# First half of the features turned and measured at the end of layer 1's attention block, with the count of fine targets between two tiles of the running count

## The chip, the cores and the metric

The kernel is one program on one core of a Trainium2 chip. The metric is device microseconds of one execution; several runs are taken and their median is compared. TensorE is called PE, VectorE DVE, ScalarE ACT, GpSimd POOL, and SyncE, which issues most transfers, SP.

## The reference

Four graph layers are applied one after the other to x (2048 nodes, 256 features, fp32), each followed by a residual and a layer norm. The adjacency matrix is 2048x2048. What matters here is the second layer (layer 1 in the code) and the start of the third:

```python
# layer 1: graph attention, 8 heads of 32 features
e = leaky_relu(s_dst[:, None, :] + s_src[None, :, :], 0.2), masked by adj
attn = softmax(e, axis=1)
h_prime = einsum('ijh,jhd->ihd', attn, Wh).reshape(n, 256)
mean, var = mean(h_prime, axis=0), var(h_prime, axis=0)      # over the 2048 nodes
h_prime = relu(gamma * (h_prime - mean) * rsqrt(var + EPS) + beta)
x = layernorm(x + h_prime)
# layer 2: only the first 64 neighbours of each node count
keep = (adj > 0) & (cumsum(adj > 0, axis=1) <= 64)
...
# layer 3: mean over all neighbours, two products, relu
```

## The kernel before, in words

Names: P = 128 partitions, T = 16 tiles of 128 nodes, KT = 2 halves of 128 features, NC = 4 column pieces of CW = 512. `edge` holds the turned adjacency matrix in fp8. `hp` (tile `cur`) is h_prime with nodes on partitions. PSUM is one tile, `banks`, of eight banks of 512 fp32 columns, shared from layer 1 on.

**Blocks.** The program is a row of blocks: `attention` (layer 0), `general_attention` for layer 0, `layer1`, `general_attention` for layer 1, and `tail` (the batch norm of layer 1, its layer norm, and layers 2 and 3). Inside a block each engine has its own instruction queue, written by hand, and waits only on semaphores. Between two blocks all five engines meet at a barrier. `general_attention` is a fallback which runs only if the number `doubt` is 1; with the given inputs each engine loads `doubt`, skips the block's body and goes on.

**End of `layer1`.** For each of 8 heads, PE makes 2 halves of 128x132 and 128x66 products (L997, L1004); the first half of the nodes sums in banks 0 to 3, the second in banks 4 to 7. DVE joins the pieces of each half (`join_pieces`, L1121), which is what frees the half's banks (semaphore `evac`, "pieces_joined"). `divide` (L1136 to L1139) divides heads 0 to 6 by their sums and writes them to `hp` while the last head is still being made; `finish_last` joins and finishes head 7 (L1149 to L1154), and makes `fine`, a column that tells whether every sum of a row is large enough. `count_fine` (L98) sums `fine` over the partitions with a product by ones, DVE turns the result into `doubt` (L1157).

**The running count.** For layer 2, `Cumulation` finds for every pair whether it is among the first 64. For tile t, PE adds `tri` x edge (`up_to_source`, L1715) to four banks, ACT compares two banks at a time through a steep Sigmoid (`compare`, L1729, two ACTIVATEs a tile), and PE then adds `above` x edge (`cumulate`, L1721) and the next tile's L1715 to the same bank. So tiles go in order around a loop ACT, PE, ACT. AHEAD = 2 tiles are compared at the end of `layer1`, the other 14 in the tail. Before the change the four banks are banks 0 to 3.

**Start of `tail`.** SP loads gamma (L1349) and beta (L1351). PE turns the first 128 features of `hp` for all nodes, 16 transposes of 128x128 fp32 into banks 4 to 7 (`turn_features`, L1364); DVE takes the statistics of each bank (`feature_stats`, L1515) and joins them (L1517); POOL takes the root of the variance (L1650, L1652); DVE makes scale and shift (`feature_factors`, L1521 to L1527); ACT applies them with Relu into `hpT` (`apply`, L1464, two ACTIVATEs a half). Then the same for the second 128 features. After that a loop over node tiles s: `back` turns `hpT` back (L1373), DVE adds the residual (L1532) and takes the layer norm, PE turns the result (L1383) and projects it (L1394), while ACT compares tile s + 6 (LEAD = 6).

ACT's queue at the start of the tail is: compare tile 2, apply the first features, compare tiles 3 to 5, apply the second features, then the loop.

## Time and profile before

| | |
|---|---|
| runs | 869.05 us median of 3 (868.21 to 869.98) |
| the profiled execution | 870.34 us |
| its span, first to last instruction | 868.6 us |
| PE busy | 810.2 us (93%) |
| DVE busy | 691.6 us (80%) |
| ACT busy | 568.3 us (65%) |
| POOL busy | 148.5 us (17%) |
| mean granted clock of TensorE | 0.988 |

The span is the time between the first and the last instruction; the execution's own time is 1.74 us longer. Busy shares are averages over all blocks. All times in rows are microseconds from the span's start; a name such as `PE banks L1364` is engine, tile written and line of the kernel before. In brackets behind an instruction stands how long its engine had been idle, and who released it.

### The profile page before, as it was taken

How to read it: one execution, taken by the hardware profiler on the slowest of the kernel's cores; microseconds unless marked ns; L12 is line 12 of the kernel's file. 1: busy time of each engine (PE TensorE's matmuls, PEld its weight loads, DVE VectorE, ACT ScalarE, POOL GpSimd, SP SyncE). 2: the span in 40 equal slices, each digit the busy share in tenths (PEclk: the TensorE clock that was granted, in tenths of full speed). 3: DMA queues.
4: the chain of work that ended last, by engine and by line, in shares of the span. 5: the costliest groups of instructions: out<-in, count | busy, mean ns of one | idle time of the engine just before them, and what ended most of it. 6: DMA issues, size and time to landing. Idle time of an engine off the chain costs nothing. (4 is left out here: it accounts for less than half of the span.)

```text
span 868.6 us, 18889 instructions
## 1 busy us (share of the span) xinstructions
PE 810.2 (93%) x7820; PEld 507.0 (58%) x7820; DVE 691.6 (80%) x1053; ACT 568.3 (65%) x568; POOL 148.5 (17%) x287
## 2 busy tenths in 40 slices
PE   3899999999999999995869999999968999999997
PEld 1334444333444434342559999999943557777786
DVE  6686989899998989897789999999943585555444
ACT  6798989897777767672369999999848630111000
POOL 2511011753110010000420000000001352111122
PEclk9999999999999999998999999999999999999999
DMA  8965344393302020001221111111000000000011
GB/s 291 263 197 169 110 137 144 95 246 85 99 16 58 1 61 1 14 1 37 85 86 52 51 32 48 32 48 48 3 1 1 1 1 1 1 1 1 2 49 49
DMA packets 28615, 56.85 MB, mean 65 GB/s; under 512 B 5808, under 2 KB 10032, under 8 KB 27120
## 3 DMA queue, kind: packets, MB, share of 16 engines
q1 hardware_dynamic: 24400, 46.19, 17.2%
q0 software_dynamic: 4128, 9.44, 4.1%
q8 instruction: 62, 1.02, 0.5%
q14 instruction: 25, 0.20, 0.1%
HBM read 38.70 MB, written 2.23 MB: 47 GB/s over the span
## 5 line engine op out<-in xcount | busy, mean ns | idle before, releaser
L484 ACT ACTIVATE ex<-scores_ps,shift 128x1024 f32<-128x1024 f32 x256 | 262.4, 1129 | 77.7 <-PE scores_ps L344 69.9
L555 DVE TENSOR_TENSOR esum<-esum,ex 128x1024 f32<-128x1024 f32 x192 | 222.9, 1211 | 7.1 <-ACT ex L484 7.1
L340 PE MATMUL scores_ps<-qst,kst 128*128 128x512 f32 x512 | 201.3, 474 | 2.9 <-ACT ex L484 2.2
L997 PE MATMUL banks<-fx,pos 128*128 128x132 f16 x2048 | 160.3, 221 | 7.1 <-DVE pos L1174 6.8
L1267 ACT ACTIVATE steps<-a_all,big_b_head 128x2048 fp8e5<-128x2048 f32 x86 | 163.6, 1988 | 0.0
L344 PE MATMUL scores_ps<-edge,negI 128*128 128x512 fp8e5 x512 | 155.3, 385 | 0.0
L340 PEld LDWEIGHTS scores_ps<-qst,kst 128*128 128x128 f32 x512 | 89.8, 189 | 70.9 <-ACT ex L484 19.8
L997 PEld LDWEIGHTS banks<-fx,pos 128*128 128x128 fp8e5 x2048 | 121.3, 98 | 8.0 <-issue 6.5
L1004 PE MATMUL banks<-fm,edge 128*128 128x66 f16 x2048 | 104.1, 193 | 0.0
L1004 PEld LDWEIGHTS banks<-fm,edge 128*128 128x128 fp8e5 x2048 | 86.6, 98 | 0.0
L1174 DVE TENSOR_TENSOR pos<-steps,edge 128x1024 int32<-128x1024 int32 (+1 forms) x65 | 77.4, 1202 | 2.4 <-PE banks L997 2.2
L344 PEld LDWEIGHTS scores_ps<-edge,negI 128*128 128x128 bf16 x512 | 29.7, 99 | 70.1 <-issue 70.1
L555 DVE TENSOR_TENSOR esum<-ex 128x1024 f32<-128x1024 f32 x32 | 38.9, 1221 | 32.8 <-ACT ex L484 32.5
L1394 PE MATMUL banks<-w,xT_ring 128*128 128x512 f32 x128 | 60.4, 594 | 0.7 <-DVE own L1558 0.6
L359 PE MATMUL mixed_total_ps<-ex,cur 128*32 128x512 f32 x512 | 58.2, 595 | 0.0
L359 PE MATMUL mixed_total_ps<-ex,v 128*32 128x512 f32 x512 | 58.2, 595 | 0.0
L1407 PE MATMUL banks<-y_halves_second,edge 128*128 128x256 f16 x512 | 56.7, 273 | 0.5 <-DVE y_halves_second L1552 0.5
L1407 PEld LDWEIGHTS banks<-y_halves_second,edge 128*128 128x128 fp8e5 x512 | 50.0, 98 | 8.7 <-issue 2.3
L284 POOL DMA_DIRECT2D qst<-high_low x56 | 27.6, 503 | 159.7 <-PE scores_ps L344 138.8
L1407 PE MATMUL banks<-y_halves,kept_rest 128*128 128x256 f16 x448 | 52.0, 273 | 0.5 <-DVE y_halves L1552 0.5
L1164 DVE TENSOR_SCALAR steps<-a_all,negb 128x2048 fp8e5<-128x2048 f32 x40 | 50.5, 1281 | 0.6 <-DMA a_all<-score_rows_dram 0.6
L1477 ACT COPY xT_ring<-banks 128x256 f32<-128x256 f32 x32 | 11.9, 371 | 57.1 <-PE banks L1383 56.8
(210 smaller groups left out, 915.5 us busy)
## 6 DMA issues: line engine op xcount, KB each, us to landing
adj_raw<-in_adjT_dram SPq DMA_DIRECT2D x32, 512.0 KB, 5.5
a_all<-score_rows_dram SPq DMA_DIRECT2D x7, 1024.0 KB, 4.7
kst<-high_low SPq DMA_DIRECT2D x56, 64.0 KB, 4.5
kst<-high_low POOLq DMA_DIRECT2D x56, 64.0 KB, 5.0
qst<-high_low POOLq DMA_DIRECT2D x56, 64.0 KB, 2.2
qst<-high_low SPq DMA_DIRECT2D x56, 64.0 KB, 3.7
ex<-in_x2T_dram SPq DMA_DIRECT2D x2, 1024.0 KB, 6.9
ex<-in_xT_dram SPq DMA_DIRECT2D x2, 1024.0 KB, 8.9
```

Of the source, the lines that this page charges most:

```text
L340: nc.tensor.matmul(to, kst[:, h, jt * P:(jt + 1) * P], qst[:, it % 2, h, :], start=True, stop=False)
L344: last = nc.tensor.matmul(to, negI[:], edge[:, jt, columns(it % NC)], start=False, stop=True)
L359: last = nc.tensor.matmul(mixed_ps[h * DH:(h + 1) * DH, :], (v0, v1)[it // NC][:, jt, h * DH:(h + 1) * DH], ex[:, s % ER, h, t * CW:(t + 1 ...
L484: nc.scalar.activation(ex[:, s % ER, h, :], scores_ps[:, u % SR, :], ACT.Exp, bias=shift[:, it // NC * HG + h:it // NC * HG + h + 1], scal ...
L555: nc.vector.tensor_tensor(esum[:, h, :], other, ex[:, s % ER, h, :], ALU.add).then_inc(summed, 1)
L997: done = nc.tensor.matmul(place(half, i), pos[:, group_of(h, k, half) % GR, jt % GU, i * P:(i + 1) * P], fx[:, e, jt].rearrange("p k r c - ...
L1004: done = nc.tensor.matmul(place(half, i)[:, C:2 * C], edge[:, jt, at:at + P], fm[:, e, jt].rearrange("p r c -> p (r c)"), start=False, sto ...
L1164: nc.vector.tensor_scalar(steps[:, pair_of(h, k) % SLOTS, jt % GU, :], aall[:, h % 2, :], negb[:, jt, one(h)], MARK, ALU.is_gt, ALU.mult, ...
L1174: nc.vector.tensor_tensor(pos[:, group_of(h, k, half) % GR, first:end, :].bitcast(int32), steps[:, pair_of(h, k) % SLOTS, first:end, at].b ...
L1267: nc.scalar.activation(steps[:, pair_of(h, k) % SLOTS, jt % GU, :], aall[:, e, :], ACT.Relu, bias=bigh[:, e, jt:jt + 1], scale=BIG, satura ...
L1394: last = nc.tensor.matmul(proj_ps[:, t % 2, :], xT[:, t % 2, k, :], (w2, w3)[layer][:, k, :], start=(k == 0), stop=(k == KT - 1))
L1407: last = nc.tensor.matmul(nb_ps[:, t % 2, 0:D], which, halves[layer][:, jt, r, :], start=(jt == 0 and r == 0), stop=(jt == T - 1 and r == 1))
```

## The change

What it does:

- A class `FeatureNorm` holds what belongs to the batch norm. Its transposes (`turn`), statistics (`take_stats`), roots (`find_root`) and factors (`factors`) are the same instructions as before.
- The first 128 features are turned at the end of `layer1`, directly behind the last product of the attention, into banks 0 to 3, in the order 3, 0, 1, 2. They need heads 0 to 3 only, which `divide` made (semaphore `heads_made`). DVE takes their statistics there too, between `fine` and the reciprocal of head 7.
- The running count moves to banks 4 to 7. So its first product waits for the join of the second half of the nodes.
- `count_fine` stands between `cumulate` of tile 0 and of tile 1. It writes column 0 of bank 3, whose statistics are taken first; after `doubt` is read, one transpose restores these 128 columns.
- gamma and beta are loaded in `layer1`, behind the pieces of the first row of scores; SP waits for them before it loads the rows of head 1.
- In the tail, POOL takes the first root at once and DVE makes the first factors. ACT applies the first features first, then compares tiles 2 to 5, then applies the second features. PE turns the second features, then cumulates tiles 2 to 5.
- The other banks of the tail change places: `back`, `turn` and `project` use banks 0 to 3, the neighbour sums banks 4 and 5, the degrees bank 6.
- The body of the fallback for layer 1 turns and measures the first features again; with the given inputs it isn't run.

```diff
@@ layer1, sync
                 sp.wait_ge(pair_landed, there)
+                feature.load(sp, gamma, beta)
@@ layer1, tensor
                 loop(pe, body)
                 pe.wait_ge(evac, LAST * 2 + 1 + EV0)
+                pe.wait_ge(heads_made, 1)
+                for b in feature.order(0):
+                    feature.turn(0, b).then_inc(feature.turned, 1)
+                pe.wait_ge(evac, LAST * 2 + 2 + EV0)
                 pe.wait_ge(count.consts, 3)
                 for c in range(NC):
-                    count.up_to_source(acc, 0, c)
+                    count.up_to_source(cum_ps, 0, c)
                 for t in range(count.AHEAD):
-                    count.cumulate(pe, acc, t)
-                count_fine(pe, nc, fine_made, ones, fine, acc[:, 7, 0:1], counted)
+                    count.cumulate(pe, cum_ps, t)
+                    if t == 0:
+                        pe.wait_ge(feature.stats, 1)
+                        count_fine(pe, nc, fine_made, ones, fine, feature.ps[:, NC - 1, 0:1], counted)
+                pe.wait_ge(counted, 2)
+                feature.turn(0, NC - 1, 1)
@@ layer1, vector, finish_last
                     nc.vector.tensor_scalar(fine[:], low, MARK * SURE, None, ALU.is_ge).then_inc(fine_made, 1)
+                    feature.take_stats(dve, 0)
                     step(nc.vector.reciprocal(over[:, :, LAST:H], sums[:, :, LAST:H]))
...
                     dve.wait_ge(counted, 1)
-                    nc.vector.tensor_scalar(doubt[:], acc[:, 7, 0:1], float(P), None, ALU.is_lt)
+                    nc.vector.tensor_scalar(doubt[:], feature.ps[:, NC - 1, 0:1], float(P), None, ALU.is_lt).then_inc(counted, 1)
@@ tail, tensor
-                for b in range(NC):
-                    turn_features(0, b)
-                count.cumulate(pe, cum_ps, count.AHEAD)
-                for b in range(NC):
-                    turn_features(1, b)
-                for t in range(count.AHEAD + 1, LEAD):
+                for b in range(NC):
+                    if b % 2 == 0:
+                        pe.wait_ge(applied, b // 2 + 1)
+                    feature.turn(1, b).then_inc(feature.turned, 1)
+                for t in range(count.AHEAD, LEAD):
                     count.cumulate(pe, cum_ps, t)
@@ tail, scalar
-                count.compare(act, cum_ps, count.AHEAD)
                 for half in range(2):
                     apply(0, half)
-                for t in range(count.AHEAD + 1, LEAD):
+                for t in range(count.AHEAD, LEAD):
                     count.compare(act, cum_ps, t)
                 for half in range(2):
                     apply(1, half)
@@ tail, vector
-                feature_stats(0)
-                dve.wait_ge(gb_landed, 16 * (1 + KT))
-                feature_factors(0)
-                feature_stats(1)
-                feature_factors(1)
+                feature.factors(dve, 0)
+                feature.take_stats(dve, 1)
+                feature.factors(dve, 1)
```

The order of ACT's instructions at the start of the tail shows more than the diff, since the table loads are put in when the program is built. ACT before, from the branch into the tail (`kept_rest` is the compare, `hp_turned` the apply):

```order
L1459 UNCONDITIONAL_BRANCH [waits barrier_Pool_Activation_PE_DVE_SP_release]
L1729 ACT_TABLE_LOAD [waits cumulated_122]
L1729 ACTIVATE kept_rest<-banks,limit 128x8x128
L1729 ACTIVATE kept_rest<-banks,limit 128x8x128 [waits cumulated_122]
L1464 ACTIVATE hp_turned<-banks,feature_scale_shift 128x1024 [waits feature_shift_241] x2
L1729 ACTIVATE kept_rest<-banks,limit 128x8x128 [waits cumulated_122] x6
L1464 ACTIVATE hp_turned<-banks,feature_scale_shift 128x1024 [waits feature_shift_241] x2
```

And in the changed kernel (L1468 is the apply, L1709 the compare):

```order
L1463 UNCONDITIONAL_BRANCH [waits barrier_Pool_Activation_PE_DVE_SP_release]
L1468 ACT_TABLE_LOAD
L1468 ACTIVATE hp_turned<-banks,feature_scale_shift 128x1024 [waits feature_factor_136] x2
L1709 ACT_TABLE_LOAD [waits cumulated_122]
L1709 ACTIVATE kept_rest<-banks,limit 128x8x128
L1709 ACTIVATE kept_rest<-banks,limit 128x8x128 [waits cumulated_122] x7
L1468 ACTIVATE hp_turned<-banks,feature_scale_shift 128x1024 [waits feature_factor_136] x2
```

The two compares of tile 2 stand behind the first apply instead of ahead of it, and there are two table loads where one was.

PE in the changed kernel, from the last product of the attention to the end of `layer1`; before, the row L1740 x16 isn't there, and L98 stands last:

```order
L1019 MATMUL banks<-fm,edge 128x66 x8
L1740 MATMUL banks<-ident,cur 128x128 [waits heads_made_200,pieces_joined_193]
L1740 MATMUL banks<-ident,cur 128x128 x15
L1695 MATMUL banks<-edge,before_in_tile 128x512 [waits count_consts_121,pieces_joined_193]
L1695 MATMUL banks<-edge,before_in_tile 128x512 x3
L98 MATMUL banks<-fine,ones 128x1 [waits fine_made_199,feature_stats_133]
L1740 MATMUL banks<-ident,cur 128x128 [waits fine_counted_198]
L918 UNCONDITIONAL_BRANCH
```

Between the fourth and the sixth of these stand the eight products of `cumulate` for tile 0, and behind L98 the eight for tile 1. The first product of the running count now stands behind 16 transposes, and one transpose behind the last.

## Rows read from the trace of the kernel before

**Rows 1.** Busy time per engine, the page's first part.

```profile
PE 810.2 (93%) x7820; PEld 507.0 (58%) x7820; DVE 691.6 (80%) x1053; ACT 568.3 (65%) x568; POOL 148.5 (17%) x287
```

**Rows 2.** Chain of waits, 644 to 662: start us, us, what.

```profile
645.23 2.50 DVE feature_stats L1515 x4
...
660.65 1.13 ACT kept_rest L1729
```

**Rows 3.** Timeline of ACT, start of the tail: start us, us, instruction, [idle before].

```profile
644.58 1.28 ACT L1729 ACT_TABLE_LOAD   x1 [3.08 <-PEq L696]
645.88 2.12 ACT L1729 ACTIVATE kept_rest<-banks,limit 128x1024 fp8e5<-128x1024 f32 x2
649.65 2.30 ACT L1464 ACTIVATE hp_turned<-banks,feature_scale_shift 128x1024 f32<-128x1024 f32 x2 [1.66 <-DVE feature_scale_shift L1527]
651.85 2.12 ACT L1729 ACTIVATE kept_rest<-banks,limit 128x1024 fp8e5<-128x1024 f32 x2
656.45 2.12 ACT L1729 ACTIVATE kept_rest<-banks,limit 128x1024 fp8e5<-128x1024 f32 x2 [0.18 <-PE banks L1715]
658.47 2.29 ACT L1464 ACTIVATE hp_turned<-banks,feature_scale_shift 128x1024 f32<-128x1024 f32 x2
```

**Rows 4.** Timeline of PE, ACT and DVE, end of layer 1.

```profile
633.68 1.02 PE L1715 MATMUL banks<-edge,before_in_tile 128*128 128x512 fp8e5 x4
633.88 1.26 DVE L1121 TENSOR_REDUCE part<-banks 128x528 f32<-128x1056 f32 x1 [0.34 <-PE banks L1004]
634.36 1.28 ACT L1729 ACT_TABLE_LOAD   x1 [8.53 <-PE banks L1715]
635.65 2.12 ACT L1729 ACTIVATE kept_head<-banks,limit 128x1024 fp8e5<-128x1024 f32 x2
636.82 0.49 PE L1721 MATMUL banks<-edge,after_in_tile 128*128 128x512 fp8e5 x1 [2.11 <-ACT kept_head L1729]
640.39 1.11 ACT L1729 ACTIVATE kept_head<-banks,limit 128x1024 fp8e5<-128x1024 f32 x1 [0.59 <-PE banks L1715]
642.43 0.28 PE L98 MATMUL banks<-fine,ones 128*128 128x1 f32 x2
642.75 0.16 DVE L1157 TENSOR_SCALAR doubt<-banks 128x1 int32<-128x1 f32 x1 [4.78 <-PE banks L98]
```

**Rows 5.** Timeline, the transposes and statistics of the first features, POOL's root.

```profile
644.56 1.94 PE L1364 MATMUL banks<-ident,cur 128*128 128x128 f32 x16 [1.85 <-PEq L696]
648.10 0.19 POOL L1650 TENSOR_TENSOR feature_scale_shift<-feature_mean_var,w_scale 128x1 f32<-128x1 f32 x1 [193.46 <-DVE feature_mean_var L1517]
```

**Rows 6.** Stretches: busy (instructions) of PE, PEld, DVE, ACT, POOL; PEclk (granted clock); DMA share; GB/s.

```profile
637.00:638.00 1.00, 1.00 (x4) 0.35 (x3) 0.93 (x3) 0.77 (x1) 0.00 (x0) 0.50 0.00 0
640.00:641.00 1.00, 1.00 (x5) 0.35 (x3) 0.00 (x0) 0.61 (x1) 0.00 (x0) 0.80 0.00 0
449.00:450.00 1.00, 0.47 (x5) 0.50 (x6) 1.00 (x3) 1.00 (x2) 0.00 (x0) 0.62 0.00 0
452.00:453.00 1.00, 0.33 (x6) 0.16 (x3) 1.00 (x2) 1.00 (x2) 1.00 (x4) 0.67 0.51 213
415.00:416.00 1.00, 1.00 (x6) 0.57 (x5) 0.97 (x4) 0.00 (x0) 0.50 (x2) 0.94 0.33 96
```

**Rows 7.** Timeline of PE, restarts after long idle stretches.

```profile
409.51 0.66 PE L943 MATMUL banks<-ident,cur 128*128 128x128 f32 x2 [6.48 <-PEq L696]
449.53 1.04 PE L997 MATMUL banks<-fx,pos 128*128 128x132 f16 x8 [4.52 <-DVE pos L1174]
```

**Rows 8.** Timeline of SP, rows of scores for heads 0 and 1; beta.

```profile
443.01 0.34 SPq L922 DMA_DIRECT2D a_all<-score_rows_dram  x1
451.09 0.33 SPq L926 DMA_DIRECT2D a_all<-score_rows_dram  x1
...
644.90 0.90 SPq L1351 DMA_DIRECT2D beta_col<-in_beta_dram  x2
```

**Rows 9.** Landing time of beta's transfers.

```profile
DMA to landing us min/median/max: 2.0/2.0/2.1
```

More of the change, by code:

```diff
@@ L807, in _ @@
                             nc.vector.tensor_tensor(to[:, g, :], to[:, g, :], (sc, pT)[g][:], ALU.add)
+                    else:
+                        dve.wait_ge(summed, U + NC)
+                        step = Chain(dve, chain, U * STEPS)
+                        for b in range(NC):
+                            step(nc.vector.bn_stats(feature.st[:, 0, b, :], feature.ps[:, b, :]))
+                        nc.vector.bn_aggr(feature.mv[:, 0, :], feature.st[:, 0].rearrange("p b s -> p (b s)"))
 def layer1(nc, S, w, ident, ones, mhalf, yT, x1, edge, wh1, score_rows, fac, efac, negb, bigb, sums, low, fine, doubt,
-           hp, pair, count, sources, ps):
+           hp, pair, count, sources, ps, feature, gamma, beta):
     TG = 4
@@ L1298, in _, with tail @@
                 for t in range(count.AHEAD):
-                    count.compare(act, acc, t)
-def tail(nc, S, gamma, beta, ident, ones, mhalf, hp, cur, edge, w2, bias2, w3, bias3, eps1, scale, count, ps, out):
+                    count.compare(act, cum_ps, t)
+def tail(nc, S, ident, ones, mhalf, hp, cur, edge, w2, bias2, w3, bias3, scale, count, ps, feature, out):
     xn = cur[:, :].rearrange("p (t d) -> p t d", d=D)
@@ L1348, in _ @@
             def _(sp):
-                sp.dma_start(gcol[:], gamma).then_inc(gb_landed, 16)
-                for k in range(KT):
-                    sp.dma_start(bcol[:, k:k + 1], beta[k * P:(k + 1) * P].rearrange("(p o) -> p o", o=1)
-                                 ).then_inc(gb_landed, 16)
                 for t in range(0, T, TD):
```

129 lines of the change are left out of this document (73 added, 56 removed).

## The prediction

> **What bounds the kernel now.** The busy times come first [rows 1]: PE is busy for 93% of the span, so on average the kernel is a PE kernel. That says nothing of the 16 us that the change touches, from the end of layer 1 to the first step of the tail's loop. The chain of waits, read there, does [rows 2]: it runs through the first features' statistics (2.50 us on DVE at 645.23), then through ACT's compares of the running count, and ends up on ACT, at the loop's first compare at 660.65. Read alone, it says that taking the statistics out must pay.
>
> The timeline of ACT in the same stretch says what lies behind this [rows 3]. From the branch into the tail ACT has nearly no idle time: table load at 644.58, compare of tile 2 at 645.88, then 1.66 us idle until the first factors, apply at 649.65, three compares, apply of the second features at 658.47. Only those 1.66 us can be won from ACT. From 660.65 on everything hangs on that queue: the first `back` waits for the second apply, and the loop's cumulate waits for compares behind it. So I count two things: when the tail begins, and how long ACT takes from its first instruction there to the start of the second apply. That is 658.47 - 644.58 = 13.89 us now.
>
> **When layer 1 ends.** Now the first product of the running count starts at 633.68, right behind the attention [rows 4]. Behind it hang in one line ACT's table load (634.36), the compares of tiles 0 and 1 (the last at 640.39), the cumulates, the fine count at 642.43 and `doubt`, which ends at 642.91.
>
> - The 16 transposes stand ahead of that first product. In the tail the same 16 took 1.94 us [rows 5]. I take +1.9 us for the line. The new wait for the second join hides: the join runs from 633.88 for 1.26 us, to 635.14 [rows 4], and the transposes end at about 635.6. Without that cover it would have cost 635.14 - 633.68 = 1.5 us, so without transposes the bank swap would be the cost.
> - The heads that they read were made before (the order shows the wait, and `divide` is far ahead of head 7's join), so that wait costs nothing.
> - The fine count moves ahead of tile 1's cumulate: it needs 0.3 to 0.5 us of PE (0.28 for its two passes, and its weight loads), and PE waits there for ACT anyway (the last compare had to wait 0.59 us for PE, so some of it may show: 0 to +0.3, taken as 0). From the line's end it takes away 642.91 - 642.43 = 0.48 us, and the restoring transpose puts back about 0.3. Net -0.2.
> - DVE gets four statistics and their join, 2.5 + 0.3 us. It sat idle for 4.78 us before `doubt` [rows 4], so they hide, with the reciprocal and product of head 7 queued behind them; nothing but the tail reads these.
> - SP's three small loads now stand behind the issue at 443.01. With issue times as in rows 8 (0.9 us for beta's two) and 2.0 us to landing [rows 9] they have landed by about 446.6; SP's next transfer is not issued until 451.09 [rows 8]. Costs nothing; without that cover 2 to 3 us of a transfer that is prefetched by a head.
>
> Layer 1 ends 1.9 - 0.2 = **1.7 us later**.
>
> **What the tail does then.** The barrier and the load of `doubt` are unchanged. For ACT: a table load at once (1.28 us), hidden behind POOL's and DVE's way to the first factors, which took 649.65 - 648.10 = 1.55 us from POOL's first instruction [rows 3, 5]. The apply then starts 1.55 us in instead of 5.07 us in. The pair of applies takes 651.85 - 649.65 = 2.20 us to the next start. Here the order shows a second table load, which was not there: 1.28 us as at 644.58, plus about 0.1 since the overlap of two neighbouring ACTIVATEs is lost. Then four compares in a row in place of three. Three took 658.47 - 651.85 = 6.62 us, one more is a round of 2.30 us (two of them from 651.85 to 656.45 are 4.60), together 8.92. Sum: 1.55 + 2.20 + 1.38 + 8.92 = 14.05 us, against 13.89: **+0.2 us**. What the change wins, the idle 1.66 us, the second table load and the new start take back. PE's 16 transposes and DVE's statistics leave the tail, but neither was waited for by anything except that idle stretch.
>
> For the table load there is a rule. By the Trainium skill ("ScalarE: Activation LUTs", section "Table sets: the hidden batching unit") Relu is in every set, so the apply needs no load of its own; the trace agrees, as the apply at 649.65 stands between two Sigmoids without one. Nevertheless the built order has one ahead of the apply at the head of the block and another for the Sigmoid, so I count both.
>
> **The clock.** PE's granted clock is at half (0.50) from 637 to 640.4 [rows 6], after an idle stretch of 2.11 us before the first cumulate at 636.82 [rows 4]. It makes the two compares of tile 1 late: at the tail's pace of 2.30 us a tile the second would have started at 639.0 and not at 640.39, so that is 1.4 us. The same gap in PE's work is still there, moved by 1.9 us, so I leave it in for the main case. New is a longer gap: PE has nothing from the end of layer 1 until the first of the applies is done, some 1.6 + 2.8 = 4.4 us. The nearest row is the gap of 4.52 us that ends at 449.53 [rows 7]: there the clock was at half from 449.4 to 452.7 [rows 6], about 3.2 us from the restart. In the tail the restart comes 2.8 us in, so half clock would last to 6.0 us in, over 16 transposes that nobody waits for, and tile 2 is compared at 6.3 us in: cost 0. The other end is the restart at 409.51, where the clock rose only in 415 to 416 [rows 6, 7], 5.6 us: that covers a tile's cumulate and costs up to 1.4 us, as in layer 1. I take +0.3, near the first.
>
> **Sum.** 1.7 + 0.2 + 0.3 = +2.2 us. Against the profiled execution's own 870.34 us that is 872.5; this execution lies 1.3 us over the median of the runs, 869.05, so for a median I forecast 869.05 + 2.2 = **871.2 us**. A measurement here can tell about 0.2%, 1.7 us, from no change.
>
> **The rivals.**
>
> 1. *The clock holds in layer 1.* With the transposes ahead, PE works 2.9 us in a row there and not 1.0 before the gap, and the gap of 1.85 us before 644.56 [rows 5] passed without a fall. Then 1.4 us come back: +0.8 us, 869.9. Against it: the gap itself is no shorter. Chance 0.27.
> 2. *The second table load costs more, or the tail's start is late.* No row shows a load right behind busy ACTIVATEs, nor POOL or DVE at work in the first microsecond of the tail. If the load costs its 1.28 us once more while ACT empties, or the half clock lasts as at 409.51, the sum is +3.5: 872.6. Chance 0.13. The Trainium skill ("ScalarE: Activation LUTs", section "What ACT_TABLE_LOAD costs") speaks for it: it states about 1.38 us of drain on top of the 1.28 us. By that figure the sum would be +3.6 us. The loads in rows 3 and 4 don't show it, since ACT was idle ahead of both and the compare starts 0.01 to 0.02 us behind the load's end.
> 3. *Faster: the chain of waits is right, and ACT's queue gives way.* If the stretch to the second apply shortens by what the first apply gains, 5.07 - 1.55 = 3.5 us, the sum is 1.7 - 3.5 = -1.8 us: 867.2. This needs the second table load to be absent or hidden and one of the four compares to fit beside other work. It decides from the point where less than 1.7 us of the 1.28 + 2.30 us that are moved behind the first apply stay on ACT. Against it stands that ACT has no idle time there to take them in. Chance 0.10.
>
> **How the numbers follow.** Main case 0.50, own range 870.3 to 872.2. Most of it (0.40) lies above +1.7 us. Slower: 0.40 + 0.13 = 0.53. The same: 0.10 of the main case, rival 1 with 0.27, and 0.03 of rival 3: 0.40. Faster: 0.07. The range 868.4 to 872.9 takes in the first rival with its clock from both sides, and half of the second, and leaves out rival 3 and the worst of rival 2.
>
> **What would show it.** In the changed profile: 16 transposes at 633.7 and the first product of the count at about 635.5; the four compares of `layer1` ending near 643.4; the tail's first instructions at about 646.2; two table loads in the tail with the second right behind the first two applies; from the first of them to the start of the second apply of features 14.0 us. The granted clock in 638 to 643 and in 648 to 653 tells rival 1 and the size of the clock's part. I am wrong if ACT's stretch is shorter than 13 us, or if the tail starts no later than 644.6.

## The result, and the profile after

The changed kernel takes 870.92 us in the median (869.06 to 872.85 in 20 runs), the kernel before 868.44 us (866.80 to 870.54 in 20 runs on the same chip). The ratio is 1.0021, 95% interval 1.0012 to 1.0030: 2.5 us slower by the medians, 1.8 us by the ratio, which is just past what can be told from no change. The forecast was +2.2 us. A few single executions of the experiments, one at 946.84 us and four above 2 ms, were in a slower state and are left out of every median below.

The profiled execution of the changed kernel took 869.06 us (span 867.3, mean clock 0.989), so it is the fastest of its 20 runs and lies 1.3 us under the profiled execution of before, which in turn is 1.9 us over its own median of 868.44. So the two profiles are not two typical executions. 1.5 us lie between them in code that the change does not touch: the last product of the attention is followed at 632.18 here and at 633.68 before [rows 4]. So both profiles are read from that point on.

Busy time per engine, the page's first part; against before [rows 1] the change adds one table load on ACT and one transpose on PE:

```profile
PE 809.1 (93%) x7821; PEld 508.5 (59%) x7821; DVE 691.7 (80%) x1053; ACT 569.4 (66%) x569; POOL 148.4 (17%) x287
```

Timeline of PE, ACT and DVE at the end of layer 1, which answers to [rows 4]: start us, us, instruction, [idle before].

```profile
632.18 1.94 PE L1740 MATMUL banks<-ident,cur 128*128 128x128 f32 x16
632.38 1.26 DVE L1144 TENSOR_REDUCE part<-banks 128x528 f32<-128x1056 f32 x1 [0.34 <-PE banks L1019]
...
633.96 1.03 PE L1695 MATMUL banks<-edge,before_in_tile 128*128 128x512 fp8e5 x4
...
634.63 1.28 ACT L1709 ACT_TABLE_LOAD   x1 [10.31 <-PE banks L1695]
...
635.50 2.48 DVE L1747 BATCH_NORM_STATS2 feature_stats<-banks 128x6 f32<-128x512 f32 x4
635.93 2.12 ACT L1709 ACTIVATE kept_head<-banks,limit 128x1024 fp8e5<-128x1024 f32 x2
637.10 0.39 PE L1701 MATMUL banks<-edge,after_in_tile 128*128 128x512 fp8e5 x1 [2.11 <-ACT kept_head L1709]
...
638.23 2.12 ACT L1709 ACTIVATE kept_head<-banks,limit 128x1024 fp8e5<-128x1024 f32 x2 [0.18 <-PE banks L1695]
...
638.97 0.28 PE L98 MATMUL banks<-fine,ones 128*128 128x1 f32 x2
639.29 0.16 DVE L1181 TENSOR_SCALAR doubt<-banks 128x1 int32<-128x1 f32 x1 [0.17 <-PE banks L98]
```

The transposes take 1.94 us and the first product of the count starts 1.78 us behind the attention instead of right behind it. The join (632.38 to 633.64) hides beside the transposes, the statistics (2.48 us) beside the count. The last thing in the line is now the restoring transpose on PE, from 641.28 to 641.55; the tail's first instruction starts 1.59 us later, against 644.58 - 642.91 = 1.67 us before.

What differs from the main case is the granted clock. Stretches of both places; columns as in [rows 6]:

```profile
638.00:639.00 1.00, 1.00 (x6) 0.52 (x6) 0.95 (x3) 0.81 (x2) 0.00 (x0) 1.00 0.00 0
640.00:641.00 1.00, 1.00 (x6) 0.31 (x4) 0.00 (x0) 0.35 (x1) 0.00 (x0) 1.00 0.00 0
...
646.00:647.00 1.00, 1.00 (x6) 1.00 (x7) 0.09 (x1) 0.98 (x2) 0.00 (x0) 0.55 0.07 16
647.00:648.00 1.00, 1.00 (x7) 1.00 (x6) 0.84 (x2) 1.00 (x1) 0.00 (x0) 0.50 0.00 0
648.00:649.00 1.00, 1.00 (x6) 1.00 (x5) 0.84 (x2) 0.99 (x2) 0.00 (x0) 0.50 0.03 8
649.00:650.00 1.00, 1.00 (x6) 0.36 (x5) 0.84 (x2) 1.00 (x2) 0.00 (x0) 0.75 0.00 0
```

The sixth number is PE's clock. In layer 1 it stays at full (2.4 GHz) behind the same gap of 2.11 us after which it had fallen before, so the two compares of tile 1 follow at the tail's pace, at 638.23 and not 1.4 us later. In the tail it is at half (1.2 GHz) behind the new gap, for about 3.4 us (0.55 in the slice from 646, 0.75 in the one from 649).

ACT, with the first instructions of PE and POOL, at the start of the tail, which answers to [rows 3, 5]:

```profile
643.14 1.28 ACT L1468 ACT_TABLE_LOAD   x1 [2.79 <-PEq L698]
643.17 0.19 POOL L1753 TENSOR_TENSOR feature_scale_shift<-feature_mean_var,w_scale 128x1 f32<-128x1 f32 x1 [190.03 <-POOLq L698]
...
644.64 2.30 ACT L1468 ACTIVATE hp_turned<-banks,feature_scale_shift 128x1024 f32<-128x1024 f32 x2 [0.22 <-DVE feature_scale_shift L1764]
...
645.90 3.53 PE L1740 MATMUL banks<-ident,cur 128*128 128x128 f32 x16 [4.35 <-ACT hp_turned L1468]
...
646.96 1.28 ACT L1709 ACT_TABLE_LOAD   x1
648.26 2.12 ACT L1709 ACTIVATE kept_rest<-banks,limit 128x1024 fp8e5<-128x1024 f32 x2
...
655.19 2.12 ACT L1709 ACTIVATE kept_rest<-banks,limit 128x1024 fp8e5<-128x1024 f32 x2 [0.18 <-PE banks L1695]
657.20 2.29 ACT L1468 ACTIVATE hp_turned<-banks,feature_scale_shift 128x1024 f32<-128x1024 f32 x2
```

ACT has no idle time to speak of. From its first instruction to the start of the second apply it takes 657.20 - 643.14 = 14.06 us, before 13.89. I call this **the stretch** from here on. From the attention's end to the tail's start it is 643.14 - 632.18 = 10.96 us here, 10.90 before. From the start of the second apply to the last instruction it is 210.1 us in both. So from the attention's end on, the two profiled executions differ by 0.2 us only: the transposes' 1.8 us were paid, 1.4 us came back from the clock in layer 1, and some 0.3 us from the fine count, which no longer stands last.

The chain of waits in the same place, start us, us, what, answers to [rows 2]:

```profile
644.64 1.21 ACT hp_turned L1468
645.90 3.53 PE banks L1740 x16
```

It now blames the 16 transposes at half clock, as it blamed the statistics before. The experiments show what that is worth.

### The profile page after: what moved, and what is told of

Same layout as the page of the kernel before. It is cut to its first block and busy times, and to the rows that moved or that the text cites. A ratio compares the mean times of both kernels' runs of the same rounds, so it can differ in the third digit from the quotient of the medians.

```text
span 867.3 us, 18893 instructions
## 1 busy us (share of the span) xinstructions
PE 809.1 (93%) x7821; PEld 508.5 (59%) x7821; DVE 691.7 (80%) x1053; ACT 569.4 (66%) x569; POOL 148.4 (17%) x287
## 3 DMA queue, kind: packets, MB, share of 16 engines
q8 instruction: 63, 1.03, 0.5%
```

## The experiments

My theory after the result: (a) layer 1's line is 1.8 us longer because the count starts later; (b) in the tail ACT's queue takes back all that the earlier apply wins, 1.4 us of it by a second table load; (c) the clock moves single executions by 1 to 2 us and the median by less. The rivals: the line is longer for another reason (the wait for the second join, DVE's statistics); the tail is bound by PE at half clock. All times below are medians, each against the runs of before on the same chip in the same set: 868.47 us for e1 to e4, 868.96 for e5 to e8, 868.38 for e9 to e12. The ratio with its interval is estimated in another way than the difference of the medians, and the two part by up to 0.7 us. The intervals are 0.9 to 1.7 us to either side, so two kernels whose differences from before lie less than some 1.5 us apart are not told apart.

**Where the line's 1.8 us come from.** The kernel before, with the count made to wait for the second join (e2):

```diff
-                pe.wait_ge(evac, LAST * 2 + 1 + EV0)
+                pe.wait_ge(evac, LAST * 2 + 2 + EV0)
```

> The kernel before with one wait changed: the first product of the running count waits for the second join as well. Theory (the line from that product to the barrier sets when layer 1 ends, with no slack): its start moves from right behind the attention to the end of the second join, 1.5 us later, and the kernel is 1.5 us slower. Rival (table load and compares have slack in layer 1): 0 to 0.5 us slower.

Measured: 870.27 us, ratio 1.0023 (1.0010 to 1.0036), +1.8 us. Timeline of ACT:

```profile
634.21 1.28 ACT L1729 ACT_TABLE_LOAD   x1 [10.05 <-PE banks L1715]
...
640.28 1.11 ACT L1729 ACTIVATE kept_head<-banks,limit 128x1024 fp8e5<-128x1024 f32 x1 [0.59 <-PE banks L1715]
```

The load waits 10.05 us here, 8.53 us before, so the later start is 1.5 us; the rest of the program is as it was (the stretch is 13.88 us). A delay of the count's first product, and nothing else of the change, costs 1.8 of the 2.5 us. The join's wait is a price of the bank swap by itself; in the changed kernel it hides under the transposes.

The changed kernel, with the first products of the count ahead of the transposes but still in banks 4 to 7 (e3):

```diff
-                pe.wait_ge(evac, LAST * 2 + 1 + EV0)
-                pe.wait_ge(heads_made, 1)
-                for b in feature.order(0):
-                    feature.turn(0, b).then_inc(feature.turned, 1)
                 pe.wait_ge(evac, LAST * 2 + 2 + EV0)
                 pe.wait_ge(count.consts, 3)
                 for c in range(NC):
                     count.up_to_source(cum_ps, 0, c)
+                pe.wait_ge(heads_made, 1)
+                for b in feature.order(0):
+                    feature.turn(0, b).then_inc(feature.turned, 1)
```

> The changed kernel with the 16 transposes behind the first four products of the count, in PE's idle gap during the table load and the first compare. Theory: the first product starts at the second join, 1.5 us behind the attention, not 1.8 to 1.9; the transposes fit into the gap of 2.1 us. 0.3 to 0.4 us faster than the changed kernel by this, and up to 1.4 us more in executions whose clock fell in that gap, since PE now works through it: +0.9 to +2.1 us against before. Rival (the transposes themselves are the cost wherever they stand): no change against the changed kernel, +2.5 us.

Measured: 870.80 us, 1.0021 (1.0009 to 1.0033), +2.3 us. No gain on the median that could be told. PE in layer 1, then PE and ACT in the tail:

```profile
636.34 1.04 PE L1694 MATMUL banks<-edge,before_in_tile 128*128 128x512 fp8e5 x4 [1.35 <-DVE part L1143]
...
648.30 3.68 PE L1739 MATMUL banks<-ident,cur 128*128 128x128 f32 x16 [4.36 <-ACT hp_turned L1467]
...
653.81 2.12 ACT L1708 ACTIVATE kept_rest<-banks,limit 128x1024 fp8e5<-128x1024 f32 x2 [1.03 <-PE banks L1694]
...
663.79 0.60 PE L1700 MATMUL banks<-edge,after_in_tile 128*128 128x512 fp8e5 x1 [1.66 <-ACT kept_rest L1708]
```

PE is idle for 1.35 us in the wait for the join, and the count starts 1.5 us behind the attention; the start gains only 0.3 us. In this execution (873.86 us) half clock lasted some 7 us in the tail (0.50 in every slice from 647 to 653), twice as long as in the changed kernel's profile. It reaches the cumulate that ACT waits for: ACT is idle for 1.03 us with both table loads in place, and the stretch is 660.44 - 645.54 = 14.90 us. The clock fell once more behind the gap of 1.66 us in the loop, which the changed kernel's profile passes at full clock (664.0 to 666.0 has 0.50 here); from the second apply to the end it is 211.7 us in place of 210.1.

The changed kernel with the banks put back: count in 0 to 3, features in 4 to 7, the transposes behind the count's first products, in the gap where PE waits for ACT (e11). The tail uses the banks as before (not in this diff); its order stays as changed.

```diff
-        cum_ps = acc[:, NC:2 * NC, :]
+        cum_ps = acc[:, 0:NC, :]
...
-                pe.wait_ge(heads_made, 1)
-                for b in feature.order(0):
-                    feature.turn(0, b).then_inc(feature.turned, 1)
-                pe.wait_ge(evac, LAST * 2 + 2 + EV0)
                 pe.wait_ge(count.consts, 3)
                 for c in range(NC):
                     count.up_to_source(cum_ps, 0, c)
+                pe.wait_ge(evac, LAST * 2 + 2 + EV0)
+                pe.wait_ge(heads_made, 1)
+                for b in feature.order(0):
+                    feature.turn(0, b).then_inc(feature.turned, 1)
```

> The changed kernel with only layer 1's part mended: the count stays in banks 0 to 3 and starts right behind the attention, the 16 transposes go into banks 4 to 7 in PE's gap behind the second join. The tail's order is the changed one, with two table loads. Theory (layer 1's line is 1.7 us of the loss): 1.7 to 2.2 us faster than the changed kernel, the more where half clock no longer falls into the gap: +0.2 to +0.7 us against before. Rival (the loss is the tail's): +1.5 us or more.

Measured: 869.37 us, 1.0007 (0.9992 to 1.0023), +1.0 us: 1.5 us of the changed kernel's 2.5 are gone (1.2 us by the ratios), a little less than expected. The tail's first instruction:

```profile
643.50 1.28 ACT L1468 ACT_TABLE_LOAD   x1 [2.79 <-PEq L698]
```

The load in layer 1 waits 8.53 us again, as before, and the stretch is 657.54 - 643.50 = 14.04 us, as in the changed kernel. The attention ends at 634.15, so the tail starts 9.35 us behind it, 1.6 us less than in the changed kernel's 10.96, with the clock at full in both. So (a) holds.

Does filling that gap bring anything by itself? The kernel before with 16 transposes there whose result nobody uses (e12; they make nothing of the output):

```diff
+                pe.wait_ge(evac, LAST * 2 + 2 + EV0)
+                pe.wait_ge(heads_made, 1)
+                for t in range(T):
+                    nc.tensor.transpose(acc[:, NC + t // NC, t % NC * P:(t % NC + 1) * P], hp[:, t, 0:P], ident[:])
                 for t in range(count.AHEAD):
```

> The kernel before with 16 transposes added in PE's idle gap at the end of layer 1 (heads 0 to 3 into banks 4 to 7, behind the second join); their result is not used and the tail turns them again as before. Pure extra work. Theory (in part of the executions the clock falls in that gap and costs up to 1.4 us, as in the profile of before): half clock is gone from there, and though the first cumulate can start up to 0.3 us later, the kernel is 0 to 0.6 us faster than before. Rival (half clock there is rare or moves on to the next gap): 0 to 0.4 us slower.

Measured: 868.47 us, 1.0006 (0.9991 to 1.0021), +0.1 us. In its profile the clock stays full in layer 1, and the tail starts 9.62 us behind the attention, not 10.90 us, yet the median is not lower. What half clock costs there in the profile of before, 1.3 us by these two, is not seen on the median. The interval reaches down to -0.8 us and not to -1.3, so it does not look as if nearly every execution of before pays this. That the median one kept its clock there, unlike the profiled one, would fit, but is not shown.

**What the tail's order is worth.** The kernel before, with only ACT's and PE's order of the change: the first apply ahead of the compare of tile 2 (e8).

```diff
-                count.cumulate(pe, cum_ps, count.AHEAD)
                 for b in range(NC):
                     turn_features(1, b)
-                for t in range(count.AHEAD + 1, LEAD):
+                for t in range(count.AHEAD, LEAD):
                     count.cumulate(pe, cum_ps, t)
...
-                count.compare(act, cum_ps, count.AHEAD)
                 for half in range(2):
                     apply(0, half)
-                for t in range(count.AHEAD + 1, LEAD):
+                for t in range(count.AHEAD, LEAD):
```

> The kernel before with one part of the change alone: in the tail ACT applies the first features ahead of comparing tile 2, and PE cumulates tile 2 behind the second features' turn. Features and count stay where they were. Theory (order alone puts a second table load and a compare behind the first apply): the first apply starts 5.1 us in as before, then 2.2, 1.4 and 8.9 us, so the stretch is 17.6 us in place of 13.89 and the kernel is 3.7 us slower. Rival (the load hides or is not needed, ACT has slack): under 2.5 us slower.

Measured: 875.02 us, 1.0072 (1.0055 to 1.0089), +6.1 us. Timeline of ACT:

```profile
643.13 1.28 ACT L1463 ACT_TABLE_LOAD   x1 [3.01 <-PEq L696]
648.26 2.30 ACT L1463 ACTIVATE hp_turned<-banks,feature_scale_shift 128x1024 f32<-128x1024 f32 x2 [3.85 <-DVE feature_scale_shift L1525]
650.58 1.28 ACT L1727 ACT_TABLE_LOAD   x1
...
660.80 2.29 ACT L1463 ACTIVATE hp_turned<-banks,feature_scale_shift 128x1024 f32<-128x1024 f32 x2
```

The stretch is 17.67 us, 3.8 more than before: the compare no longer fills the wait for the factors (3.85 us idle), and the second load is there. So the new order is a loss that the early statistics must first make good; they win 17.67 - 14.06 = 3.6 us. The profiled execution, 872.68 us, is the fastest of the six, and outside the stretch it is as before (10.89 us from the attention's end to the tail, 210.1 us behind the second apply), so it bears out the 3.7 us expected. The median's further 2.3 us are not settled.

The changed kernel, with the tail's order as before (e1: compare of tile 2 first, its cumulate ahead of the second transposes):

```diff
+                count.cumulate(pe, cum_ps, count.AHEAD)
...
+                count.compare(act, cum_ps, count.AHEAD)
                 for half in range(2):
                     apply(0, half)
-                for t in range(count.AHEAD, LEAD):
+                for t in range(count.AHEAD + 1, LEAD):
```

> The changed kernel with ACT's and PE's order in the tail as before: compare tile 2, then the first apply; cumulate tile 2, then turn the second features. Theory (the tail's start is bound by ACT's queue, and the second table load and the moved compare ate the gain): one table load at the head of the tail, ahead of the Sigmoid; from it to the start of the second apply 1.3 + 2.0 + 2.2 + 6.6 = 12.2 us in place of 14.06, so 1.9 us faster than the changed kernel and +0.6 us (0.0 to +1.1) against the kernel before. Rival (the loss comes from layer 1 and the clock alone, ACT's queue has slack): the end moves by under 0.5 us, +2.0 to +2.5 against before.

Measured: 870.47 us, 1.0019 (1.0007 to 1.0030), +2.0 us. ACT and PE:

```profile
631.89 1.94 PE L1742 MATMUL banks<-ident,cur 128*128 128x128 f32 x16
...
644.43 1.28 ACT L1711 ACT_TABLE_LOAD   x1 [2.85 <-PEq L698]
...
646.89 0.52 PE L1703 MATMUL banks<-edge,after_in_tile 128*128 128x512 fp8e5 x1 [4.12 <-ACT kept_rest L1711]
...
653.18 2.12 ACT L1711 ACTIVATE kept_rest<-banks,limit 128x1024 fp8e5<-128x1024 f32 x2 [1.14 <-PE banks L1697]
```

One load, and the apply follows the compare at 647.73 without idle time, but the stretch is 13.08 us and not 12.2: the clock is at half from 647 to about 650.4, now under the cumulate that ACT waits for, and ACT stands idle for 1.14 us. This profile also shows layer 1's part once more. The clock fell behind its gap here, as in the profile of before, and from the attention's end to the tail it is 644.43 - 631.89 = 12.54 us against 10.90: 1.6 us more, the same as with the clock at full in both.

The changed kernel with one table load (e10), by a Sigmoid of 128x1 put first in ACT's tail, so that the set of the compares is the one that is loaded:

```diff
+                nc.scalar.activation(tiny[:], count.limit[:], ACT.Sigmoid)
                 for half in range(2):
                     apply(0, half)
```

> The changed kernel with one tiny Sigmoid (128x1) added as ACT's first instruction of the tail, so that the Sigmoid's table is loaded at the tail's start and the Relu runs under it: the second table load is gone and nothing else moves. Theory: the stretch is 12.7 to 12.9 us in place of 14.06 (1.3 us less, the tiny Sigmoid's 0.2 us lying under the wait for the factors), and the kernel is 1.1 to 1.3 us faster than the changed one: +1.1 to +1.4 against before. Rival (PE at half clock then keeps the compares waiting instead): under 0.6 us of it remains, +1.9 or more.

Measured: 870.45 us, 1.0032 (1.0018 to 1.0045), +2.1 us, 0.4 less than the changed kernel by the medians and 1.0 more by the ratios: not told apart. ACT:

```profile
644.03 1.28 ACT L1489 ACT_TABLE_LOAD   x1 [2.79 <-PEq L698]
645.32 0.20 ACT L1489 ACTIVATE tiny<-limit 128x1 f32<-128x1 f32 x1
...
651.98 2.12 ACT L1711 ACTIVATE kept_rest<-banks,limit 128x1024 fp8e5<-128x1024 f32 x2 [2.14 <-PE banks L1697]
```

The load is gone, and a wait of 2.14 us for PE stands in its place: the 16 transposes take 3.68 us at half clock, then comes the cumulate of tile 2. In this execution the stretch is even longer, 658.60 - 644.03 = 14.57 us.

**Keeping PE at work.** The first transposes of the features are repeated at the start of the tail, pure extra work into the same banks, and the apply waits for them (e5; `WARM` = 3 banks of 4 here, 12 transposes):

```diff
+                for b in range(WARM):
+                    feature.turn(0, b).then_inc(warmed, 1)
...
                 def apply(k, half):
+                    act.wait_ge(warmed, WARM)
```

> The changed kernel, in whose tail PE turns three banks of the first features once more at the start (12 transposes, the same numbers into the same place, which the first apply waits for). Adds work, takes away PE's new idle stretch of 4.4 us: PE works for 1.4 us right at the tail's start, as it did before. Theory (the long gap brings half clock into the tail in most executions, and this is the clock's part of the loss): no half clock in the tail's first 8 us, ACT's stretch from its first table load to the second apply stays 14.06 us, and the median falls by 0.3 to 1.0 us against the changed kernel: +1.5 to +2.2 us against before. Rival (the clock's part is nothing, the restart is covered): the same as the changed kernel, +2.4.

Measured: 872.68 us, 1.0049 (1.0030 to 1.0068), +3.7 us. ACT tells why:

```profile
649.33 1.28 ACT L1474 ACT_TABLE_LOAD   x1 [4.35 <-DVE feature_scale_shift L1770]
```

With a second semaphore to wait for, the load was put behind that wait, where nothing hides it: the stretch counted from PE's restart at 647.81 is 15.36 us. The same with the wait on DVE, ahead of the last factor, and the load back in its place (e9):

```diff
-                    act.wait_ge(warmed, WARM)
...
+        if k == 0:
+            dve.wait_ge(self.warmed, WARM)
         dve.wait_ge(self.factor, 3 * k + 2)
```

> As e5, with the wait for the repeated transposes moved from ACT to DVE's last factor: in e5 ACT's second wait drew the first table load behind the factors (idle 4.35 us ahead of it), which cost 1.3 us of its own, so e5 said nothing of the clock. The added work may hold the first apply by up to 0.2 us. Theory (half clock in the tail is part of the loss): the granted clock is full in the tail's first 8 us, the stretch is 14.1 to 14.3 us, and the median falls to +1.2 to +2.2 us against before. Rival (the tail's half clock is covered by the table load and the first compare in nearly all executions): as the changed kernel, +2.4 us, or +2.6 with the hold.

Measured: 870.96 us, 1.0031 (1.0018 to 1.0043), +2.6 us, so no gain on the changed kernel. The clock stays full over the tail's start and the second transposes take 2.19 us, as before the change, but the stretch is 660.22 - 645.90 = 14.32 us, 0.26 more than in the changed kernel, since the apply starts later. So half clock of 3.4 us, as in the changed kernel's profile, is covered by the load and the compare beside it, whatever the chain of waits says. The cover is narrow: the same tail with half clock of some 7 us, in e3's profile, took 0.84 us more.

All 16 transposes repeated, on top of the tail's order as before (e6, on e1's kernel of 870.47 us). Here the compare stands first in ACT's queue, so the load has no second wait ahead of it:

```diff
+WARM = 4
...
+                for b in range(WARM):
+                    feature.turn(0, b).then_inc(warmed, 1)
...
                 def apply(k, half):
+                    act.wait_ge(warmed, WARM)
```

> e1 with the transposes of the first features made once more at the tail's start (16, 1.9 us). In e1 the tail's stretch was 13.1 us and not 12.2, with ACT idle for 1.14 us behind a cumulate and a turn at half clock. Theory (that idle time was the clock's): half clock gone, the stretch is 12.2 us, 0.9 us faster than e1: -0.3 to +0.7 us against before, what is left being layer 1's 1.7 us less the tail's 1.7. Rival (PE's order, cumulate then turn, keeps tile 3 waiting at any clock): as e1, +1.6 us.

Measured: 868.40 us, 0.9992 (0.9981 to 1.0003), -0.6 us. Timeline of ACT:

```profile
645.08 1.28 ACT L1717 ACT_TABLE_LOAD   x1 [2.85 <-PEq L699]
...
652.87 2.12 ACT L1717 ACTIVATE kept_rest<-banks,limit 128x1024 fp8e5<-128x1024 f32 x2 [0.19 <-PE banks L1703]
...
657.19 2.29 ACT L1475 ACTIVATE hp_turned<-banks,feature_scale_shift 128x1024 f32<-128x1024 f32 x2
```

The stretch is 12.11 us, as was reckoned for one load and no idle time: 1.0 us less than without the extra work. The median is 2.6 us lower, each against its own before (2.3 us by the ratios). More work on PE made the kernel faster. That the time fell by more than the one profile's 1.0 us fits executions in which half clock lasts longer, as in e4 below, but is not shown.

**Both mended.** Count in banks 0 to 3 with the transposes in the gap (as in e11), and the tail's order as before (e4); in the tail, against the changed kernel:

```diff
+                count.cumulate(pe, cum_ps, count.AHEAD)
...
+                count.compare(act, cum_ps, count.AHEAD)
                 for half in range(2):
                     apply(0, half)
-                for t in range(count.AHEAD, LEAD):
+                for t in range(count.AHEAD + 1, LEAD):
```

> The changed kernel with the count kept in banks 0 to 3 and the features in banks 4 to 7 (other banks of the tail as before), the transposes behind the first products of the count, and the tail's order as in e1. Theory: the count starts right behind the attention as before, the transposes go into the gap from the second join on (they end about 0.3 us behind the first cumulate's old start), the fine count is off the line's end: layer 1 ends 0 to 0.2 us later or earlier; the tail's ACT stretch is 12.2 us against 13.89. Together 1.7 us faster than before, up to 2.5 us where the clock no longer falls in the gap. Rival (the tail needs the second features' factors later than it needs ACT, or PE's gap opens elsewhere): 0 to 0.5 us faster.

Measured: 867.52 us, 0.9985 (0.9975 to 0.9995), -0.9 us, where -1.7 was expected. The stretch is 14.00 us in its profile and not 12.2, with ACT idle for PE, and PE at half behind the tail's gap for some 7 us:

```profile
644.40 0.61 PE L1703 MATMUL banks<-edge,after_in_tile 128*128 128x512 fp8e5 x1 [4.12 <-ACT kept_rest L1711]
...
651.62 2.12 ACT L1711 ACTIVATE kept_rest<-banks,limit 128x1024 fp8e5<-128x1024 f32 x2 [2.07 <-PE banks L1697]
```

And with the 16 repeated transposes at the tail's start (e7):

```diff
+WARM = 4
...
+                for b in range(WARM):
+                    feature.turn(0, b).then_inc(warmed, 1)
...
                 def apply(k, half):
+                    act.wait_ge(warmed, WARM)
```

> e4 with the transposes of the first features made once more at the tail's start. e4's stretch in the tail was 14.0 us, of which 2.07 us ACT waited for PE at half clock. Theory: without half clock the stretch is 12.2 us, 1.8 us less than e4's profile and about 1 us less in the median, so 1.7 to 2.5 us faster than before (0.2 to 0.3%). Rival as in e6: as e4, 1.2 us faster than before.

Measured: **866.27 us, 0.9971 (0.9959 to 0.9984), -2.7 us**, the best of all, 5.2 us under the changed kernel, each against its own before. ACT, and a stretch of PE's clock:

```profile
644.33 1.28 ACT L1717 ACT_TABLE_LOAD   x1 [2.86 <-PEq L699]
...
647.63 2.31 ACT L1475 ACTIVATE hp_turned<-banks,feature_scale_shift 128x1024 f32<-128x1024 f32 x2
...
652.13 2.12 ACT L1717 ACTIVATE kept_rest<-banks,limit 128x1024 fp8e5<-128x1024 f32 x2 [0.19 <-PE banks L1703]
...
656.45 2.29 ACT L1475 ACTIVATE hp_turned<-banks,feature_scale_shift 128x1024 f32<-128x1024 f32 x2
```

```profile
648.00:649.00 1.00, 0.94 (x5) 0.31 (x4) 0.00 (x0) 1.00 (x2) 0.00 (x0) 1.00 0.00 0
```

The stretch is 12.12 us, the clock full.

The parts beside the time, for all kernels. Each part is from one profile, so it goes with that execution's clock; the attention's end is the start of its last group of products plus 0.24 us, as in the profile of before. "Clock" says whether the granted clock stayed full behind the gap in layer 1, and at the start of the tail.

| kernel | attention's end, at | from there to the tail, us | stretch, us | second apply to the end, us | clock in layer 1 | clock in the tail | us against before |
|---|---|---|---|---|---|---|---|
| before | 633.68 | 10.90 | 13.89 | 210.1 | fell | full | 0 |
| changed | 632.18 | 10.96 | 14.06 | 210.1 | full | half, 3.4 us | +2.5 |
| e1, compare first | 631.89 | 12.54 | 13.08 | 210.2 | fell | half, 3.4 us | +2.0 |
| e2, before with the join's wait | 632.01 | 12.45 | 13.88 | 210.2 | fell | full | +1.8 |
| e3, count first | 634.83 | 10.71 | 14.90 | 211.7 | full | half, 7 us | +2.3 |
| e4, both mended | 632.52 | 9.42 | 14.00 | 210.2 | full | half, 7 us | -0.9 |
| e5, 12 transposes, load late | 635.28 | 12.53 | 15.36 | 211.6 | fell | full | +3.7 |
| e6, compare first, 16 transposes | 632.81 | 12.27 | 12.11 | 210.1 | fell | full | -0.6 |
| e7, both mended, 16 transposes | 634.91 | 9.42 | 12.12 | 210.2 | full | full | -2.7 |
| e8, before with the changed order | 632.24 | 10.89 | 17.67 | 210.1 | fell | half, 3.4 us | +6.1 |
| e9, 12 transposes | 633.69 | 12.21 | 14.32 | 210.1 | fell | full | +2.6 |
| e10, one load | 633.07 | 10.96 | 14.57 | 210.1 | full | half, 7 us | +2.1 |
| e11, layer 1 mended | 634.15 | 9.35 | 14.04 | 210.1 | full | half, 3.4 us | +1.0 |
| e12, before with the gap filled | 633.11 | 9.62 | 13.89 | 210.2 | full | full | +0.1 |

Three things can be read from it. The change moves what it was said to move and nothing behind the second apply. With the clock alike, its line in layer 1 is 1.6 us longer (10.96 against 9.35 at full clock, 12.54 against 10.90 where it fell). And the attention's end, in code that is the same in all of them but for three small loads and a semaphore, lies anywhere from 631.89 to 635.28, which is more than any single part of the change.

## Why the prediction was right

The size (+2.2 us, measured +2.5 by the medians and +1.8 by the ratio) and the sign held, and so did the two terms that do not hang on the clock: 1.6 us in layer 1 (1.7 said) and 0.2 us in ACT's stretch (0.2 said). Together they are 1.8 us. The clock's part is the open end. The main case left it as in the profile of before in layer 1 and put +0.3 on the tail. Whether the median execution of either kernel is such a one is not shown, and e12 speaks against it for the kernel before. So the agreement of +2.2 with +2.5 to the tenth is in part luck.

- *Layer 1 ends 1.7 us later.* Right as a difference at the same clock. The 16 transposes take 1.94 us, the start moves 1.8 us (1.9 said), and from the count's start to the tail it is 0.1 us less in e1 than before, both with the clock fallen (10.76 against 10.90; 0.2 said). Delaying the count alone costs 1.8 us, and putting it back wins 1.5 us. The join hides under the transposes as said; bare it delays the start by 1.5 us, as said. DVE's statistics and their join are done at 638.27, long before the tail, where POOL's first instruction starts 0.03 us behind ACT's. SP issued gamma's load at 441.81 and beta's two at 442.28, and its next transfer only at 449.60, so waiting for them delayed nothing.
- *ACT's stretch 14.05 us.* 14.06, and by its terms: load to apply 644.64 - 643.14 = 1.50 (1.55 said), applies and second load 648.26 - 644.64 = 3.62 (2.20 + 1.38 = 3.58 said), four compares 657.20 - 648.26 = 8.94 (8.92 said). This was the step that kept the forecast from turning to faster, and it rested on the order of the built program: the diff does not show the second load.
- *The clock, +0.3 us.* Its place and the gap (4.35 us, 4.4 said) were right, and by the stretches half clock lasted some 3.4 us, from 646.1 to 649.5, about what was read from the restart at 449.53 (3.2 us from there; the fall itself lies nearer 449.2 than 449.4 by its row's 0.62, which changes nothing). It cost nothing in that profile, as said. The other end, put at up to 1.4 us, was seen as well: half clock of some 7 us in the same tail cost 0.84 us (e3). How often it lasts that long is not known, so the 0.3 is neither borne out nor refuted. What I did not see is that the load and half clock lie side by side: a single load alone (e10) and a full clock alone (e9) win nothing that can be told. The order as before together with the extra transposes (e6) is 3.0 us faster than the changed kernel by the medians. It also moves a compare and a cumulate, though; the changed order with a single load and the extra transposes was not run.
- *The sign of being wrong, "the tail starts no later than 644.6",* came up: the tail starts at 643.14 in the changed profile. It was given as a time in the profile, and 1.5 us of it are the attention's earlier end. Of the rest, 10.96 us against 10.90 from there on, the clock in layer 1 gave back what the transposes took. So by this profile alone the step in layer 1 would have counted as refuted. It stands by the profiles with the clock alike.
- *Rival 1, the clock holds in layer 1,* came true in the profiled execution. Its reason does not hold: it says that PE works for 2.9 us in a row before the gap and not 1.0, but before the change as well the count follows on the attention without a break [rows 4], and with the same transposes ahead the clock fell in e1 and e5 at once and in e6 and e9 within about 1.4 us of the restart. The changed kernel's 20 times lie in two groups, 9 from 869.06 to 870.03 at mean clocks of 0.985 to 0.989, 11 from 870.89 to 872.85 at 0.982 to 0.987. Rival 1's 869.9 lies with the first, my 871.2 with the second. That the gap in layer 1 parts them is not shown. e11, with that gap filled, still spreads over 4.1 us, and the attention's end alone moves by 3.4 us between profiles.
- *Rival 2, a dearer table load or a late start,* fell for both of these. Its third way, half clock as long as at 409.51 (5.6 us from the restart), nearly came in the profiles of e3, e4 and e10 (4.8 to 5.3 us), so it was a live one. The load starts 0.02 us behind the end of busy ACTIVATEs (644.64 + 2.30 = 646.94, load at 646.96) and the compare 0.02 us behind the load's end. The switch costs 3.62 - 2.20 = 1.42 us in all. The Trainium skill ("ScalarE: Activation LUTs", section "What ACT_TABLE_LOAD costs") gives 1.28 us for the load, which the rows show to the digit, and some 1.38 us of drain on top. The rows disagree with the second: 1.42 us for the whole switch, where the two would make 2.66. The measurement decides.
- *Rival 3, faster,* fell: the stretch did not shorten. Its mechanism is sound, though, and needs what it named, a single load and a compare that fits beside other work, and the third thing that it did not name, a PE at full clock. With all three the stretch is 12.1 us.

## What to carry to other kernels

Count the stretch of the queue that sets the end, not the wait that you take away: if the instructions put ahead of or behind the freed place are as long as the wait, nothing is won, and a table load may come with the new order. Put moved work into a gap that exists on its engine (here PE's wait behind the first count, once the banks allow it) and not ahead of the line that everything hangs on. And where two costs lie side by side, an experiment that removes one may show nothing: remove both before you call either free. Compare profiles part by part from a common point, with the clock alike. Here single profiles differ by more than the change itself in code that it does not touch.

## What the runs showed of the hardware

- **Extra PE work can pay.** The 16 repeated transposes fill PE's gap at the tail's start. Without such work there the granted clock is at 0.50 for 3 to 7 us around the end of gaps of 4.1 to 4.4 us in all seven profiles that have them. With it the clock stays at 1.00 there, and the time falls by 2.6 us (e1 to e6) and by 1.7 us (e4 to e7). In the changed order (e9) nothing was won.
- **A gap of 2.11 us can cost the clock or not.** In nine profiles PE has that gap in layer 1. Behind it the clock stayed full in two (changed, e10) and fell to half in seven, with nearly the same code. In the five in which transposes stand in the gap (e3, e4, e7, e11, e12) it stayed full. At the same code the way to the tail took 10.96 us with it and 12.21 to 12.54 us without. On the median of e12 this gain did not show.
- **One profile is one draw.** The same kernel's runs spread over 3.7 us, and a profiled execution can lie 2.3 us under its kernel's median (e8, 872.68 against 875.02) or 3.8 us over it (e5, 876.51 against 872.68).
- **Where a table load stands is set by the waits of the instruction behind it.** With one semaphore to wait for (e9), the load stood ahead of the wait and was hidden; with two (e5) it stood behind and put its 1.28 us on ACT's way.
